# Moving the three-relation layers' edge sort and adjacency counts under the first layer's relation units

## The reference

```
h = relu(layernorm(x)); x = x + L0(h)   # 34 relations: per-relation mean of neighbours times W_rel[r], plus h @ W_root, then a GCN layer
h = relu(layernorm(x)); x = x + L1(h)   # two GCN layers
h = relu(layernorm(x)); x = x + L2(h)   # three RGCN layers of 3 relations; h gets 128 columns of a node-type embedding
h = relu(layernorm(x)); x = x + L3(h)   # one GCN layer
```

## Time and profile before

| what | value |
|---|---|
| median of 3 runs | 1968.68 us (1967.73 to 1973.69) |
| the profiled execution's own time | 1970.0 us |
| its span | 1968.2 us |
| mean granted TensorE clock | 0.924 |
| PE busy | 1697.2 us (86%) |
| DVE busy | 1169.7 us (59%) |
| ACT busy | 594.1 us (30%) |
| POOL busy | 360.0 us (18%) |

### The profile page before, as it was taken

How to read it: one execution, slowest core, us unless ns; L and a number is a source line. 1 busy time by engine, 2 the same in 40 slices (tenths; PEclk the granted TensorE clock), 3 DMA queues, 4 the chain that set the end, 5 groups by cost and what they waited for, 6 DMA issues and landing times. The chain is left out here.

```text
span 1968.2 us, 30246 instructions
## 1 busy us (share of the span) xinstructions
PE 1697.2 (86%) x10272; PEld 1632.7 (83%) x10273; DVE 1169.7 (59%) x1804; ACT 594.1 (30%) x782; POOL 360.0 (18%) x301
## 2 busy tenths in 40 slices
PE   2652955499999999999975898999999999899988
PEld 2541844499999999999975898899988999899988
DVE  8677779566776766776644547255433454444463
ACT  0112000255554555554533222122112222222221
POOL 1005120144454444554430000000000000000000
PEclk9675976699999999999987998999999999999999
DMA  1003100489898988998864011222112221121111
GB/s 66 4 26 111 32 10 1 159 248 258 238 271 217 283 229 221 276 269 222 239 138 125 27 57 49 71 82 81 37 32 73 73 72 53 54 80 54 39 48 48
DMA packets 84463, 230.04 MB, mean 117 GB/s; under 512 B 10327, under 2 KB 22618, under 8 KB 84411
## 3 DMA queue, kind: packets, MB, share of 16 engines
q1 hardware_dynamic: 65066, 158.14, 25.2%
q0 software_dynamic: 19344, 71.18, 15.4%
HBM read 190.01 MB, written 39.28 MB: 116 GB/s over the span
## 5 line engine op out<-in xcount | busy, mean ns | idle before, releaser
L1062 PE MATMUL layers_ps_o<-layers_w_hi,layers_g_hi 128*125 128x384 f32 (+1 forms) x1040 | 361.7, 348 | 5.6 <-DVE layers_w_lo L926 4.4
L1063 PE MATMUL layers_ps_o<-layers_w_lo,layers_g_hi 128*125 128x384 f32 (+1 forms) x1040 | 360.2, 346 | 0.0
L1064 PE MATMUL layers_ps_o<-layers_w_hi,layers_g_lo 128*125 128x384 f32 (+1 forms) x1040 | 359.6, 346 | 0.0
L1656 DVE TENSOR_TENSOR l_means_w_lo<-l_means_w_raw,l_means_w_hi 128x768 fp32r<-128x768 f32 x209 | 198.4, 961 | 130.2 <-ACT l_means_w_hi L1602 130.2
L1087 PE MATMUL layers_ps_g<-a,h_hi 125*128 125x316 f32 x840 | 198.1, 318 | 47.2 <-DVE h_lo L554 34.3
L1735 PE MATMUL l_means_ps_y<-l_means_w_hi,l_means_g_hi 128*128 128x384 f32 x912 | 231.7, 334 | 0.0
L1735 PE MATMUL l_means_ps_y<-l_means_w_lo,l_means_g_hi 128*128 128x384 f32 x912 | 231.4, 334 | 0.0
L1735 PE MATMUL l_means_ps_y<-l_means_w_hi,l_means_g_lo 128*128 128x384 f32 x912 | 231.4, 334 | 0.0
L1602 ACT CAST l_means_w_hi<-l_means_w_raw 128x768 fp32r<-128x768 f32 x209 | 174.6, 837 | 186.5 <-PE l_means_ps_y L1735 186.5
L1062 PEld LDWEIGHTS layers_ps_o<-layers_w_hi,layers_g_hi 128*125 128x125 f32 x1040 | 193.6, 186 | 16.0 <-issue 6.2
L1064 PEld LDWEIGHTS layers_ps_o<-layers_w_hi,layers_g_lo 128*125 128x125 f32 x1040 | 193.3, 186 | 5.4
(11 more groups left out here) (282 smaller groups left out, 2470.2 us busy)
## 6 DMA issues: line engine op xcount, KB each, us to landing
l_means_w_raw<-in_L_gnn_W_rel SPq DMA_DIRECT2D x210, 384.0 KB
layers_w_raw<-in_L_gnn_w_rel SPq DMA_DIRECT2D x39, 384.0 KB, 3.4
layers_w_raw<-in_L_gnn_w_rel SPq DMA_DIRECT2D x21, 448.0 KB, 3.8
layers_a_raw<-adj SPq DMA_DIRECT2D x9, 769.0 KB
layers_w_raw<-in_L_gnn_W SPq DMA_DIRECT2D x18, 384.0 KB, 5.2
l_means_list_now<-targets SPq DMA_DIRECT2D x35, 192.0 KB
layers_w_raw<-in_L_gnn_w_root SPq DMA_DIRECT2D x13, 384.0 KB, 3.9
layers_w_raw<-in_L_gnn_w_root SPq DMA_DIRECT2D x7, 448.0 KB, 4.1
```

What stands on the lines that cost most here:

```text
L1062: t.matmul(out, g_hi[:, f, rows], w_hi[:, f, cols], start=(f == 0), stop=False)
L1063: t.matmul(out, g_hi[:, f, rows], w_lo[:, f, cols], start=False, stop=False)
L1064: mm = t.matmul(out, g_lo[:, f, rows], w_hi[:, f, cols], start=False, stop=(f == fc - 1))
L1656: v.tensor_tensor(w_lo[:, f, :], w_raw[:, f, :], w_hi[:, f, :].bitcast(F32), ALU.subtract)\
```

## The change

The stages `s2_sort` and `s2_build` are gone. Their work is spread as follows (line numbers are those of the kernel after):

- x, the zero rows, the row statistics and the normalised h move to the head of the `s0_sort` stage (`normalise_rows`). The load of x is split in 112 and 13 partitions.
- `root_rows` waits for h; its first three weight loads are issued ahead of the store of h, not behind it.
- In `add_means` DVE first works out where each edge goes (`positions`), for 30 keys (relation, source tile, half of the target columns). Then unit by unit: 17 units do 5 edge columns each (`columns`) with 5 matmuls more on PE, 15 units count two keys each (`key_onehots` on DVE, `count_key` on PE, `copy_key` on ACT), 2 units do nothing more. A key has as many slots of 128 edges as it needs (no lots of 6), each with one one-hot pair of 125 and 315 columns and one matmul. With the edges of the reference's inputs that is 94 slots over the 30 keys.
- The results of a unit's three tiles are packed in five PSUM banks in place of six; the eighth bank (`ps_b`) holds the lists and counts. A product that was two matmuls of 384 columns is now 512 and 256.
- ACT scales all y tiles (before, DVE took tiles 0 and 2).
- The sums for `adj_all` and the embedding columns of h come at the end of `add_means`, the store of `adj2` behind the last unit's weight loads on SP.

```diff
+def normalise_rows(nc, ctx, block, sem, x_dram, x, h, ident, spare_rows):
...
+        rows = x_dram.rearrange("(k p) f -> p k f", p=NP)
+        for part in (slice(0, 112), slice(112, NP)):
+            sp.dma_start(x[part], rows[part]).then_inc(x_loaded, 16)
+        sp.wait_ge(spare_ready, 1)
+        sp.dma_start(spare_rows.rearrange("(t p) f -> p t f", p=SLOT),
+                     spare[:].unsqueeze(1).broadcast_to([SLOT, UNIT, width])).then_inc(spare_stored, 16)
+        sp.wait_ge(spare_stored, 16)
...
@@ root_rows, sync
-        sp.dma_start(store_first.rearrange("(k p) f -> p k f", p=NP), h[:, :, 0:width]).then_inc(rows_stored, 16)
         for f in range(fc):
+            if f == RING:
+                sp.wait_ge(rows_normal, 1)
+                sp.dma_start(store_first.rearrange("(k p) f -> p k f", p=NP), h[:, :, 0:width]).then_inc(rows_stored, 16)
...
@@ add_means, sync
+            sp.wait_ge(key_copied, keys + 1)
+            sp.dma_start(second.adj.rearrange("(t k) p c -> p (t k) c", t=second.kinds),
+                         cnt.rearrange("p (t a) c -> p t (a c)", a=2)).then_inc(adj_stored, 16)
             sp.wait_ge(w_loaded[fc - 1], 16 * end + 16)
             sp.sem_inc(waited, 1)
+            sp.wait_ge(adj_stored, 16)
@@ add_means, scalar
+                def take_y(tiles):
+                    act.wait_ge(w_used, fc * u + fc)
+                    act.wait_ge(y_free, u + 1)
+                    for j in range(tiles):
+                        ins = nc.scalar.activation(y[:, j, :], ps_y[j], ACT.Copy,
+                                                   scale=row_inv[:, bass.ds(UNIT * u + j, 1)])
+                    ins.then_inc(y_ready, 2)
@@ add_means, vector
+            def columns(n):
+                dve.wait_ge(columns_used, n + 1)
+                at = bass.ds(COLUMNS * n, COLUMNS)
+                v.tensor_tensor(is_slot[:], slot_iota[:], slot_of[:, at].unsqueeze(1).broadcast_to([EP, SLOT, COLUMNS]),
+                                ALU.is_equal)
+                for c in range(COLUMNS):
+                    col = bass.ds(COLUMNS * n + c, 1)
+                    for i in range(2):
+                        ins = v.tensor_scalar(is_tile[:, c, i, :], tile_iota[:], hi[:, col], loads[:, i, col],
+                                              ALU.is_equal, ALU.mult)
+                ins.then_inc(columns_ready, 1)
+            def key_onehots(k):
+                first, end = tiles_of(dve, k)
+                with dve.Fori(first, end) as n:
+                    i = tile_number(n)
+                    dve.wait_ge(onehots_free, i + 1)
+                    at = bass.ds(i, 1)
+                    v.tensor_scalar(is_src[:, i % ONEHOTS, :], node_iota[:, 0:NP], slot_src2[:, at], None, ALU.is_equal)
+                    v.tensor_scalar(is_dst[:, i % ONEHOTS, :], node_iota[:], slot_dst2[:, at], None,
+                                    ALU.is_equal).then_inc(onehots_ready, 1)
@@ add_means, tensor
+            def count_key(k):
+                pe.wait_ge(key_copied, k + 1)
+                t.matmul(ps_b[0:NP, 0:2], zeros[:, 0:NP], zeros[:, 0:2], start=True, stop=False, skip_group_check=True)
+                first, end = tiles_of(pe, k)
+                with pe.Fori(first, end) as n:
+                    i = tile_number(n)
+                    pe.wait_ge(onehots_ready, i + 1)
+                    t.matmul(ps_b[0:NP, 0:HALF], is_src[:, i % ONEHOTS, :], is_dst[:, i % ONEHOTS, :],
+                             start=False, stop=False, skip_group_check=True).then_inc(onehots_free, 1)
+                t.matmul(ps_b[0:NP, 0:2], zeros[:, 0:NP], zeros[:, 0:2], start=False, stop=True, skip_group_check=True)\
+                    .then_inc(key_counted, 1)
...
+            with pe.Fori(0, list_units) as n:
+                one_unit(unit(n))
+                columns(n)
+            t.matmul(ps_b[:, 0:2], zeros[:], zeros[:, 0:2], start=False, stop=True, skip_group_check=True)\
+                .then_inc(lists_summed, 1)
+            pe.wait_ge(lists_taken, 2)
+            with pe.Fori(0, key_units) as n:
+                one_unit(unit(n + list_units), n)
+                count_key(key_number(2 * n + 1))
+            with pe.Fori(list_units + key_units, count(pe)) as n:
+                one_unit(unit(n))
```

More of the change, by code:

```diff
@@ L1 @@
+from collections import namedtuple
 from contextlib import ExitStack
@@ L71, in semaphores, with sort_edges @@
     return sem
-def sort_edges(nc, tag, src, dst, etype, keys, lot, slot_src, slot_dst, counts=None, lots=None, tile_of=None,
-               beside=None, aside=None):
+def sort_edges(nc, tag, src, dst, etype, keys, lot, slot_src, slot_dst, lots, tile_of, first, aside):
     slots = slots_of(keys, lot)
-    by_tile = tile_of is None
     chunk = 17
@@ L1413, in _, with add_means @@
             t.transpose(ps_x[0:UNIT * u_max - 128, 1, 0:SLOT], flat[:, 128:UNIT * u_max], ident[:]).then_inc(lists_turned, 1)
-def add_means(nc, tag, units, w_rel, rows, sums, plan, src_index, slot_dst, row_index, row_inv, targets):
+HALF = NC // 2
+ONEHOTS = 8
+COLUMNS = 5
+Background = namedtuple("Background", "src dst etype kinds adj adj_all ident h node_types emb")
+def add_means(nc, tag, units, w_rel, rows, sums, plan, src_index, slot_dst, row_index, row_inv, targets, second):
     width = rows.shape[1]
@@ L1426, in add_means @@
     half = width // 2
+    keys = second.kinds * NT * 2
+    tiles2 = E // SLOT + keys + 1
+    list_units = EC // COLUMNS
+    key_units = keys // 2
+    assert EC % COLUMNS == 0 and list_units + key_units <= w_rel.shape[0] and 2 * tiles2 <= 256
     with ExitStack() as ctx:
@@ new lines, in add_means @@
+        key_iota = sb("key_iota", [EP, keys], F32)
+        slot_iota = sb("slot_iota", [EP, SLOT, COLUMNS], F16)
+        tile_iota = sb("tile_iota", [EP, tiles2], F16)
+        node_iota = sb("node_iota", [SLOT, HALF], F16)
+        zeros = sb("zeros", [SLOT, SLOT], F16)
+        zero = sb("zero", [EP, 1], F32)
+        ones = sb("ones", [EP, EP], F16)
+        lower = sb("lower", [EP, EP], F16)
+        hi = sb("hi", [EP, EC], F32)
+        slot_of = sb("slot_of", [EP, EC], F16)
+        loads = sb("loads", [EP, 2, EC], F32)
@@ L1471, in unit, with tile_number, key_number, tiles_of @@
             return nc.s_assert_within(u, 0, units - 2, skip_runtime_bounds_check_because="units - 1 bounds their number")
+        def tile_number(i):
+            return nc.s_assert_within(i, 0, tiles2 - 1, skip_runtime_bounds_check_because="all edges fit tiles2 tiles")
+        def key_number(k):
+            return nc.s_assert_within(k, 0, keys - 1, skip_runtime_bounds_check_because="two keys for each of key_units units")
+        def tiles_of(eng, k):
+            first = eng.value_load(counts[0:1, 0, bass.ds(k, 1)], min_val=0, max_val=tiles2 - 1)
+            number = eng.value_load(counts[0:1, 1, bass.ds(k, 1)], min_val=1, max_val=tiles2)
+            return first, first + number
         def has_third(eng, u):
```

536 lines of the change are left out of this document (291 added, 245 removed).

## The result

The changed kernel takes 1988.57 us (median of 4 runs, 1986.67 to 1992.52), the kernel before 1968.57 on the same chip: a ratio of 1.01, 95% interval 1.0088 to 1.0113. Forecast were 1881 us. The profiled execution has a span of 1988.7 us, and the forecast's sum meant 1880.8, so 107.9 us are to be found.

What follows compares the result with a forecast made beforehand. PE was taken to set the pace in `add_means` and the layers, but not in the first three stages. Terms summed to -87.4 us: profiled 1970.0 to 1882.6, median 1881 us; range 1864 to 1920.

Steps and rivals of the forecast that it cites:

- cast of the sort: Front: without the first sort and counts, the second sort's first cast stands at 22, not 162.6; -140.6 us.
- rest of that stage: Sort stage behind the cast: earlier root weights and fewer DVE/POOL collisions bring PE's sort matmuls sooner; -7 us, 0 to -14.
- list units: 17 units of `add_means`: five more matmuls of 228 columns each on PE, 85 x 0.11; +9.4 us.
- lists to keys: Between 17th and 18th unit: PE waits for DVE's lists, then loads a register with nothing queued; +2.5 us.
- counting units: matmuls, sequencer, y: 15 counting units: slot and small matmuls +17.3, PE's loads and loops +5, ACT scaling y alone +1.
- end of `add_means`: Counts' store behind SP's last weight load shares engines with the last scatters, y 0.9 us later; +3 us, 0 to 8.
- the disputed price: Counting units: PE's register loads and one-matmul loops stay nearly hidden under queued matmuls; +5 us, bounds 0 and 48.
- upper bound of 3.2 us a unit: Counting units, queue of nine: 0.5 per key, 2 x 0.7 for loops, 1.3 at the border; 48 us over 15 units.
- A: Rival: PE's queue holds only nine matmuls, so holes show at each key and border; +43, 1924 us; chance 0.12.
- B: Rival: DVE's unhidden register loads make it the bound in counting units; 1927 us; chance 0.17, whole or half.
- C: Rival: slower, nothing hidden in counting units on PE or DVE, list units paying 1.3 each; 2085 us; chance 0.02.
- D: Rival: better front, splits and casts never meet and `positions` is at its low end; 1864 us; chance 0.12.

Runs made afterwards that it cites:

- e5: Changed kernel plus 14 unread matmuls in each counting unit, 7 ahead of the second key's count and 7 behind it; 1967.22 us.
- e4: Changed kernel with PE's count of each key replaced by one fixed matmul without loads or loop, DVE's one-hot work kept; 1895.61 us.
- e7: Changed kernel with GpSimd's root-weight splits from the second on held until VectorE's small first-sort operations are done; 1986.52 us.
- e6: Against the changed kernel: four slots per key, written out on PE and DVE, counts ahead of the fifth and sixth product rows; 1904.96 us.
- e9: Changed kernel, loads and loops kept, with a unit's two counts placed apart, ahead of the third and sixth product rows; 1936.80 us.

## Why the prediction was wrong, term by term

| term | forecast | measured |
|---|---|---|
| cast of the sort (162.61 before) | -140.6 | -138.7 |
| rest of that stage | -7 | -0.7 |
| `plan_units` | 0 | +0.5 |
| `positions` to PE's first matmul | +22 | +22.4 |
| list units | +9.4 | +11.8 (17 x 0.69) |
| lists to keys | +2.5 | +7 (2.4, and the stop of 4.55) |
| counting units: matmuls, sequencer, y | +23.3 | +111.4 (402.23 - 286.29 - 4.55) |
| end of `add_means` | +3 | +8.4 |
| layers | 0 | -1.5 |

**The step that failed is "the disputed price"**, the +5 "near the bottom, since a border shows no hole at all". 88 of the 108 us are there. The row was read rightly, the place was not. The border of the earlier trace rows stands behind the 72 wide products of its unit; the second key stands behind twelve, and between these and its loads stands a wait for ScalarE's copy, past which the sequencer can't run ahead. The price itself stood in the earlier trace rows, 2.0 us for two loads when little is queued, and it came back as 2.04. The upper bound of 3.2 us a unit was too low as well: it had 0.35 us a turn where the timeline shows 0.8, and nothing for the clock. The shown unit's 6.0 us over the forecast are, in this order: second key and border, 4.24 instead of 0.58, 3.7; the half-clock sums, 5.91 us instead of the 4.41 of e5, 1.5; the first key 1.11 instead of 0.58, 0.5; 0.3 unassigned.

**The rivals.** A named the right mechanism (the sequencer pays, holes at each key and border) and gave it 43 us and 0.12. Its reason, a queue of nine, isn't what the runs show: behind sixty wide matmuls two loads and three turns, by estimate 4.4 us of the sequencer (2.0 and three of 0.8), cost 0.5, where nine matmuls are 1.6 us. By the Trainium skill, "TensorE: Matmul & The Clock Gate", in its table, that queue is 64 deep. No run here shows how deep it is. At the second key its depth didn't matter: the wait let through no more than the twelve ahead of it. B fell (e4, and VectorE busy 14.04 of 23.96 us). C, "decides from 93 us more", had the right sign and about half of its mechanism: the counting units, not the list units and not VectorE; its chance of 0.02 was far too small. D did not come.

**The clock** was in no term. Of the 15 counting units of the changed kernel, 14 were followed by sums that ran wholly or partly at 1.2 GHz (a mean granted clock of 0.50 to 0.80 over their first 2 us), the one before 990.55 by sums at 2.4. With the holes filled (e5) it was 1.00 behind all of them. In `s2_build` that had been visible: the earlier trace rows show a key at half clock.

**The front** came within 1.9 us: x landed at 11.5 in place of 9.5, all DMA engines busy (1.00) at 285 GB/s where 412 were assumed. "DVE finds POOL busy in its larger operations, not in all four small ones" was wrong, one small one was enough. While VectorE's scan ran (28.15 to 35.43), GpSimd's split took 7.66 us for 1.8; then GpSimd's splits followed without a pause from 38.75 to 54.44, and VectorE's operation ended with them, at 54.48:

```profile
29.36 7.66 POOL L526 TENSOR_TENSOR root_w_lo<-root_w_raw,root_w_hi 128x768 fp32r<-128x768 f32 x1
...
52.65 1.79 POOL L526 TENSOR_TENSOR root_w_lo<-root_w_raw,root_w_hi 128x768 fp32r<-128x768 f32 x1
```

The Trainium skill, "SBUF — State Buffer", on the shared port pair, says it is a lock held for a whole instruction, whose loser blocks; the traces agree as to the blocking, with 14.21 us against 0.18 (e7). It speaks of one instruction, though, and here VectorE was passed over by eight splits that began behind the one it met. Why it got in between them in e7 (1.3 to 1.7 us each) and not here stays open.

**Right**: `positions`, the list units nearly, the layers untouched, and that PE and not VectorE bounds a unit, though it is PE's sequencer where the forecast had its array. e6, with no hole left and the clock up, has counting units of 18.4 us where 17.9 were forecast for one slot a key less, so the sum was sound once its premise held.

## What to carry to other kernels

"No hole at this border" is a statement on what stands queued ahead of the border, not on the price of a branch or a register load. Before moving such code, count the array time between the last semaphore wait of the engine and the new place, and set the sequencer's own time (here 2.0 us for two loads, 0.8 a turn, 1.6 for a unit's border) against it. Leave a margin: in e9 the count ahead of the third row still had holes. Place counts, loops and loads with wide work behind them as well as ahead, write short loops out where their length can be bounded, and add to each remaining hole what the clock takes back afterwards.

## What was not expected of the hardware

- More matmuls made the kernel faster: 210 unread ones, 21.4 us less (e5).
- Entering the counting loop for the first time stopped PE for 2.14 and then 4.55 us (7.70 at once in e6) with no wait. The "instruction" DMA queue, without a packet from 500 to 580 us, moved 2 packets (0.03 MB) between 585 and 596. The Trainium skill, "Runtime: NRT & Kernel Launch", on instruction fetch, says that a branch to a place outside the loaded window waits for a fetch. The trace fits it; no run here tried it.
- A VectorE operation on 34 columns took 14.21 us beside GpSimd's splits.
